# Attention sums with the weighted rows standing still and narrow one-hots moving, turned back in pairs of destination tiles

## The chip, the cores and the metric

The kernel runs on one core of one Trainium2 chip. The metric is the device time of one execution in microseconds (us). Engines are called by their names in the profile: PE (TensorE), with its weight loads as PEld, DVE (VectorE), ACT (ScalarE), POOL (GpSimd) and SP (SyncE). A measurement of this kernel is the median of several runs.

## What is computed

Four graph layers over 6,250 nodes and 100,000 edges, sorted by destination, each added to the running state. The change touches the third, an attention layer with eight heads, then a feed-forward network and two layer norms:

```python
h = (x @ W_gat).reshape(n, H, C)
a_s = jnp.sum(h * att_src, axis=-1); a_d = jnp.sum(h * att_dst, axis=-1)
e = a_s[src] + a_d[dst]
e = jnp.where(e >= 0, e, NEG_SLOPE * e)
m = jax.ops.segment_max(e, dst, num_segments=n)
alpha = jnp.exp(e - m[dst])
den = jax.ops.segment_sum(alpha, dst, num_segments=n)
alpha = alpha / den[dst]
agg = jax.ops.segment_sum(h[src] * alpha[..., None], dst, num_segments=n)
h1 = _layernorm(x + agg.reshape(n, H * C) + b_gat, ln1_g, ln1_b)
out = _layernorm(h1 + jax.nn.relu(h1 @ W1 + b1) @ W2 + b2, ln2_g, ln2_b)
```

What matters here is the last `segment_sum`: for every destination node the sum of its edges' weighted rows (128 numbers), of their eight weights, and, for the self-loop, the segment's maximum (eight more).

## The kernel before

The edges are cut into 782 tiles of 128 (`TILES`), the nodes into 49 tiles of 128 (`NT`). Since edges are sorted, a tile of 128 edges covers about eight nodes; the kernel allows each tile a reach of 26 to 64 nodes around its expected place (`reach_of`), and `near(tile)` lists the one or two node tiles that this reach touches. The attention goes in 56 batches (`ABATCHES`) of 14 edge tiles (`AB`), in two halves of seven (`AH`).

In one batch b the engines do this. POOL gathers the 14 tiles of source rows by indirect DMA into a ring of three batches (L1017); a slot is free again when the weighted rows of batch b-3 are made. SP loads per-edge flags (L694) and rows of destination numbers (L701). ACT copies the gathered scores into `stage` (L1286). PE turns them (L1876); DVE scans them forward and back for the segment maxima (L2550, L2551), PE fetches the neighbours across rows (L1887, L1888), DVE joins (L2555 to L2557), PE turns back (L1894, L1895). `expand` (L1809) brings node scores to the edges through one-hots made by `by_dst` (L2530, L2531), and DVE sums those pieces (L2561). Then DVE makes the exponents (L2567 to L2573), ACT the exponentials (L1325 to L1327), and DVE the weighted rows, 128 numbers a row (L2580), beside which lie the eight weights and eight maxima: 144 columns, `WL2`.

`by_edge` (L2538) makes, on DVE, for each edge tile a one-hot of 256 columns: the edge's destination modulo 256. It runs twice a batch, for seven tiles each. `aggregate` (L1828) on PE multiplies for each tile and each node tile near it: the 128 columns of the one-hot that belong to this node tile are loaded as the standing operand, the 144 columns of the weighted rows move, and the product (128 nodes by 144) adds up in bank `ps[i % 2]`. When the last edge tile near node tile i is through, ACT copies the sum to `Dw` (L1293, `agg_out`).

PE's order is written by hand: in the iteration of batch b it takes, for k from 0 to 13, the `expand` of tiles 2k and 2k+1 of batch b (for k under 7) and the `aggregate` of tile k of batch b-1. The fetch across rows stands behind k = 2, the turning back behind k = 5. So from k = 7 on an iteration holds `aggregate` alone, and DVE meanwhile makes exponents and weighted rows. DVE's order in a batch is: scans, joins, `by_edge` of half 0, the two sums of `expand`, exponents, `by_edge` of half 1, weighted rows, `by_dst` for the next batch, and then one or more steps of `residual`: for each group of seven node tiles (r = 0 to 6) a step called self, exp, mix, sum, stats, root, stand, norm, gain, one iteration after the other from iteration 8r+10 on. The feed-forward of finished groups runs within iterations 32 to 54 too (`FF_AT`). What is left of `residual` follows behind the last batch.

After the attention stand ten steps of the fourth layer, which the change does not touch.

## Time and profile before

| | us |
|---|---|
| median of 3 runs | 4953.56 |
| lowest and highest run | 4930.44, 4966.02 |
| span of the profiled execution | 6157.9 |
| the same, between first and last gather of the attention (L1017) | 1352.4 |

The profiled execution is 1204 us longer than the median run. Its rows give durations and who waits for whom; what a stretch takes in an execution that isn't profiled has to be argued. In the page's 40 slices the attention is 14 to 22; PE, DVE and POOL are each busy for about half of it. In the ten steps behind it PE stands at 8 tenths or more.

### The profile page before, as it was taken

To read this page: it belongs to the slowest core of one execution; us is meant where nothing else is said; L and a number is where in the kernel's file an instruction comes from. 1 tells how busy PE (TensorE), PEld (TensorE's weight loads), DVE (VectorE), ACT (ScalarE), POOL (GpSimd) and SP (SyncE) were. 2 spreads that over 40 slices of the span, in tenths; PEclk is the share of its full clock that TensorE was granted. 3 is DMA by queue.
4 is the path that set the end of the run, shared out by engine and by line. 5 is a ranking of instruction groups with operands and counts; after the bars stand their busy time and mean duration, and the time that the engine had idled before them with its cause. 6 is when DMAs were issued, how large, how long until landed. Compare 5 with 4: busy or idle time off the path is not lost.

```text
span 6157.9 us, 72323 instructions
## 1 busy us (share of the span) xinstructions
PE 4502.8 (73%) x25760; PEld 2814.8 (46%) x25760; DVE 2553.7 (41%) x8838; ACT 1022.9 (17%) x2922; POOL 3237.6 (53%) x3390
## 2 busy tenths in 40 slices
PE   3778477888775445446555788988888898888888
PEld 2556355566554334344444343434443444444344
DVE  6778444445443445555567422222222222222222
ACT  4656311111111000001222200000000000000001
POOL 3232365566555555555553365565656556565655
PEclk8888688899887666667767999989999999999999
DMA  5222222122222222222221555555555555555554
GB/s 136 77 83 79 77 56 52 51 58 59 55 55 57 67 70 75 68 68 69 65 71 42 160 173 159 171 158 164 172 167 164 166 178 166 161 174 161 165 170 135
DMA packets 455501, 686.46 MB, mean 111 GB/s; under 512 B 91793, under 2 KB 237879, under 8 KB 455120
## 3 DMA queue, kind: packets, MB, share of 16 engines
q1 hardware_dynamic: 341188, 454.71, 23.5%
q0 software_dynamic: 107584, 223.83, 14.0%
q8 instruction: 210, 3.44, 0.2%
q10 hardware_dynamic: 6364, 3.20, 0.2%
q14 instruction: 155, 1.27, 0.1%
HBM read 599.50 MB, written 82.31 MB: 111 GB/s over the span
## 4 chain that ended last, share of the span: by engine, by line
PE 42%; another core or an unknown queue 24%; DVE 18%; issue 11%; ACT 3%; DMA 1%; ACTq 0%; SPq 0%; DVEq 0%; POOL 0%; POOLq 0%
PE ps L2007 27%; PE ps L1751 5%; DVE E L2458 4%; DVE B L2538 2%; PE pt L2102 2%; DVE arena L2580 1%; PE ps L1828 1%; PE ps L2093 1%; PE pt L2038 1%; PE ps L2022 1%; DVE O L3023 1%; PE pt L1719 1%; ACT E L1561 1%; DVE scores L3019 1%
## 5 line engine op out<-in xcount | busy, mean ns | idle before, releaser
L2007 PE MATMUL ps<-arena,E 128*128 128x512 fp8e4 (+1 forms) x4900 | 1147.0, 385 | 93.6 <-issue 84.8
L2007 PE MATMUL ps<-arena,A 128*128 128x512 fp8e4 (+1 forms) x4900 | 1142.1, 385 | 62.4 <-issue 60.1
L1052 POOL DMA_INDIRECT arena<-table,src_i x810 | 776.9, 959 | 685.7 <-DMA table<-E 255.0
L1017 POOL DMA_INDIRECT E<-gat_table,src_i x782 | 759.3, 971 | 634.6 <-DVE arena L2580 367.7
L1052 POOL DMA_INDIRECT arena<-x_spill,src_i x810 | 775.3, 957 | 579.0 <-issue 225.8
L1002 POOL DMA_INDIRECT arena<-table,src_i x782 | 742.8, 950 | 583.5 <-issue 217.1
L1751 PE MATMUL ps<-E,arena 128*128 128x352 f32 (+22 forms) x2932 | 783.6, 421 | 241.1 <-DVE E L2458 155.4
L2007 PEld LDWEIGHTS ps<-arena,E 128*128 128x128 f16 x4900 | 471.4, 100 | 648.6 <-issue 193.9
L2007 PEld LDWEIGHTS ps<-arena,A 128*128 128x128 f16 x4900 | 472.9, 100 | 608.9 <-issue 154.8
L1751 PEld LDWEIGHTS ps<-E,arena 128*128 128x128 f32 x2932 | 515.4, 211 | 441.4 <-issue 195.5
L2909 DVE SCALAR_TENSOR_TENSOR C<-ps,sc_b,scores 128x128 f32<-128x128 f32 x490 | 138.9, 345 | 1295.1 <-PE ps L2022 769.3
L1828 PE MATMUL ps<-arena,B 128*128 128x144 f32 x2244 | 512.4, 376 | 62.4 <-issue 61.8
L2458 DVE SCALAR_TENSOR_TENSOR E<-arena,pt 128x512 f32<-128x512 bf16 (+5 forms) x782 | 480.6, 674 | 175.3 <-remote 85.7
L1828 PEld LDWEIGHTS ps<-arena,B 128*128 128x128 f32 x2244 | 415.1, 250 | 85.3 <-issue 83.1
L2102 PE MATMUL pt<-arena,E 128*128 128x258 f16 x1911 | 312.5, 286 | 67.8 <-ACT E L1561 45.2
L1087 POOL DMA_INDIRECT A<-first_rows,src_i x162 | 163.1, 1007 | 360.6 <-PE pt L2077 263.7
L1494 ACT ACTIVATE O<-ps 128x512 f32<-128x512 f32 x100 | 58.6, 586 | 1731.7 <-remote 920.3
L1561 ACT ACTIVATE E<-ps 128x490 fp8e4<-128x490 f32 (+1 forms) x507 | 299.0, 597 | 195.4 <-remote 122.2
L2895 DVE TENSOR_SCALAR rows<-w_gat,dst_f 128x54 f16<-128x54 bf16 (+17 forms) x966 | 155.5, 249 | 388.7 <-remote 251.4
L1876 PE MATMUL pt<-ident,E 128*128 128x128 f32 x56 | 23.9, 427 | 382.2 <-ACT E L1286 275.0
L3023 DVE TENSOR_SCALAR O<-arena 128x245 bf16<-128x245 bf16 x1014 | 233.4, 284 | 114.5 <-remote 75.0
L2093 PE MATMUL ps<-O,scores 128*128 128x245 bf16 x1014 | 201.2, 282 | 69.2 <-ACT E L1561 49.6
(350 smaller groups left out, 4557.6 us busy)
## 6 DMA issues: line engine op xcount, KB each, us to landing
arena<-adj SPq DMA_DIRECT2D x180, 1024.0 KB
arena<-adj SPq DMA_DIRECT2D x90, 1088.0 KB
adj<-E SPq DMA_DIRECT2D x39, 784.0 KB
arena<-table,src_i POOLq DMA_INDIRECT x1592
O<-dst_rows SPq DMA_DIRECT2D x112, 224.0 KB
arena<-adj SPq DMA_DIRECT2D x20, 768.0 KB
x_spill<-A SPq DMA_DIRECT2D x55, 256.0 KB
arena<-x_spill,src_i POOLq DMA_INDIRECT x810
```

Of the source, the lines that this page charges most:

```text
L1002: pool.indirect_dma_start(out=rows_ring[:, k % RING, :], out_offset=None, in_=table, in_offset=bass.IndirectOffsetOnAxis(ap=src_i[:, k:k + ...
L1017: pool.indirect_dma_start(out=att_rows[:, b % 3 * AB + at, :], out_offset=None, in_=gat_table, in_offset=bass.IndirectOffsetOnAxis(ap=src_ ...
L1052: pool.indirect_dma_start(out=y_rows[:, g % ERING, k, :], out_offset=None, in_=(table, x_spill)[half], in_offset=bass.IndirectOffsetOnAxis ...
L1087: pool.indirect_dma_start(out=rows0[:, x % (2 * EG0), :], out_offset=None, in_=first_rows, in_offset=bass.IndirectOffsetOnAxis(ap=src_i[:, ...
L1561: act.activation(made[:, i % MADE, :, 2 * BD * q:2 * BD * q + w], ps[pair % 4][:, 0:w * NT].rearrange("p (d j) -> p j d", j=NT), ACT.Copy, ...
L1751: mm = pe.matmul(ps[m % 4][:, (lo - WD * m) * BASES:(hi - WD * m) * BASES], rows_ring[:, k % RING, :], m_ring[:, k % MS, lo - first_dst(k) ...
L1828: mm = pe.matmul(ps[i % 2][:, 0:WL2], edge_hot[:, (2 * b + half) % 3, k % AH, i % 2 * P:(i % 2 + 1) * P], weighted_rows[:, b % 2, k, :], s ...
L2007: mm = pe.matmul(chunk_banks[n % 2][:, 0:len(some) * P], y[:, i, h * D:(h + 1) * D], adj_ring[:, piece % ADJ_RING, 0:len(some), at:at + P] ...
L2093: pe.matmul(ps[pair % 4][:, h * BW:(h + 1) * BW], hot_src[:, g % SRC, :], hot_code[:, g % HOT, 0:BW], start=True, stop=True).then_inc(sem( ...
L2102: mm = pe.matmul(bank0_of(m)[:, 0:2 * LO], made[:, m % MADE, j, :], y16[:, j, :], start=(j == 0), stop=(j == NT - 1))
L2458: dve.scalar_tensor_tensor(m_ring[:, k % MS, w, :], bc(iota_h[:, w], BASES), dst_rel[:, k:k + 1], row_bc(made_c[:, c % 2, at, :], w.stop - ...
L3023: dve.tensor_scalar(hot_code[:, g % HOT, 0:BW], iota_w[:, 0:BW], slot_c[:, g // P, g % P:g % P + 1], None, ALU.is_equal).then_inc(sem("hot ...
```

## The change

The product in `aggregate` is turned round. The weighted rows of an edge tile are now the standing operand, and a one-hot of at most 64 columns (`WD`), the window of destinations that the tile can reach, moves. It comes out as 128 features by at most 64 nodes, and 16 rows (weights and maxima) by as many nodes, which are two matmuls: one with the 128 feature columns standing (L1860 of the changed kernel) and one with the 16 columns beside them (L1864). Both are cut where the window crosses a boundary of 256 nodes (`window_parts`), since a bank of 512 columns now holds a pair of node tiles: columns 0 to 255 the features, columns 256 to 511 the 16 rows.

`by_edge` makes seven one-hots of 64 columns in one instruction (L2594) from `dst_in_window`, the destination relative to the window, which is copied once; before these were seven instructions of 256 columns.

When a pair is through, ACT copies the bank to SBUF in two pieces (`agg_keep`), PE turns it back in two or four transposes (`turn_back`, at k = 6 and k = 11) into `pt[0]`, and ACT copies 288 columns to `Dw` (`agg_out`). In all 25 pairs. The steps of `residual` all come one iteration later.

```diff
@@ buffers @@
-        edge_hot = B[:, 0:3 * AH * 2 * P].rearrange("p (s t d) -> p s t d", s=3, t=AH)
+        edge_hot = B[:, 0:3 * AH * WD].rearrange("p (s t d) -> p s t d", s=3, t=AH)
+        dst_in_window = B[:, 2048:2048 + ET]
+        agg_in, agg_beside_in = B[:, 3072:3072 + 2 * P], B[0:2 * HEADS, 3072 + 2 * P:3072 + 4 * P]
@@ helpers @@
+        def window_parts(tile):
+            lo, hi = max(reach_of(tile)[0], 0), min(reach_of(tile)[1], NP)
+            ends = [lo, *range(lo // (2 * P) * 2 * P + 2 * P, hi, 2 * P), hi]
+            return [(a // (2 * P), a % (2 * P), b - a, a - first_dst(tile)) for a, b in zip(ends, ends[1:])]
+
+        PAIRS = (NT + 1) // 2
+        pair_first, pair_last = ([end(k for k in range(TILES) if c in [part[0] for part in window_parts(k)])
+                                  for c in range(PAIRS)] for end in (min, max))
+
+        def pairs_ended(b, half):
+            return [c for c in range(PAIRS) if pair_last[c] // AB == b and pair_last[c] % AB // AH == half]
+
+        def pair_width(c):
+            return min(2, NT - 2 * c)
+
...
+        agg_back = pt[0][:, WL2:3 * WL2]
...
-        RESIDUAL = {"self": 10, "exp": 11, "mix": 12, "sum": 13, "stats": 14, "root": 15, "stand": 16, "norm": 17, "gain": 18}
+        RESIDUAL = {"self": 11, "exp": 12, "mix": 13, "sum": 14, "stats": 15, "root": 16, "stand": 17, "norm": 18, "gain": 19}
@@ ScalarE @@
+                def agg_keep(b, half):
+                    for c in pairs_ended(b, half):
+                        n = pair_width(c) * P
+                        act.wait_ge(sem("aggregated"), pair_last[c] + 1)
+                        if c:
+                            act.wait_ge(sem("agg_turned"), c)
+                        act.activation(agg_in[:, 0:n], ps[c % 2][:, 0:n], ACT.Copy)
+                        act.activation(agg_beside_in[:, 0:n], ps[c % 2][0:2 * HEADS, 2 * P:2 * P + n], ACT.Copy
+                                       ).then_inc(sem("agg_kept"), 1)
+
                 def agg_out(b, half):
-                    for i in range(NT):
-                        if near_last[i] // AB == b and near_last[i] % AB // AH == half:
-                            act.wait_ge(sem("aggregated"), near_last[i] + 1)
-                            act.activation(Dw[:, i * WL2:(i + 1) * WL2], ps[i % 2][:, 0:WL2], ACT.Copy
-                                           ).then_inc(sem("agg_out"), 1)
+                    for c in pairs_ended(b, half):
+                        n = pair_width(c) * WL2
+                        act.wait_ge(sem("agg_turned"), c + 1)
+                        act.activation(Dw[:, 2 * c * WL2:2 * c * WL2 + n], agg_back[:, 0:n], ACT.Copy
+                                       ).then_inc(sem("agg_out"), 1)
 
...
-                    agg_out(b - 1, 0)
+                    agg_keep(b - 1, 0)
                     if b < ABATCHES:
                         act.wait_ge(sem("exponents_made"), b + 1)
...
-                    agg_out(b - 1, 1)
+                    agg_out(b - 2, 1)
+                    agg_keep(b - 1, 1)
+                    agg_out(b - 1, 0)
...
+                agg_out(ABATCHES - 1, 1)
@@ TensorE @@
-                    for i in near(tile):
-                        if tile == near_first[i] and i >= 2:
-                            pe.wait_ge(sem("agg_out"), i - 1)
-                        mm = pe.matmul(ps[i % 2][:, 0:WL2],
-                                       edge_hot[:, (2 * b + half) % 3, k % AH, i % 2 * P:(i % 2 + 1) * P],
-                                       weighted_rows[:, b % 2, k, :],
-                                       start=(tile == near_first[i]), stop=(tile == near_last[i]))
+                    parts = window_parts(tile)
+                    for c, at, n, col in parts:
+                        if tile == pair_first[c] and c >= 2:
+                            pe.wait_ge(sem("agg_kept"), c - 1)
+                        pe.matmul(ps[c % 2][:, at:at + n], weighted_rows[:, b % 2, k, 0:D],
+                                  edge_hot[:, (2 * b + half) % 3, k % AH, col:col + n],
+                                  start=(tile == pair_first[c]), stop=False, skip_group_check=True)
+                    for c, at, n, col in parts:
+                        mm = pe.matmul(ps[c % 2][0:2 * HEADS, 2 * P + at:2 * P + at + n], weighted_rows[:, b % 2, k, D:WL2],
+                                       edge_hot[:, (2 * b + half) % 3, k % AH, col:col + n],
+                                       start=False, stop=(tile == pair_last[c]), skip_group_check=True)
                     mm.then_inc(sem("aggregated"), 1)
+
+                def turn_back(b, half):
+                    for c in pairs_ended(b, half):
+                        pe.wait_ge(sem("agg_kept"), c + 1)
+                        if c:
+                            pe.wait_ge(sem("agg_out"), c)
+                        for k in range(pair_width(c)):
+                            pe.transpose(agg_back[:, k * WL2:k * WL2 + D], agg_in[:, k * P:(k + 1) * P], ident[:, :])
+                            mm = pe.transpose(agg_back[:, k * WL2 + D:(k + 1) * WL2], agg_beside_in[:, k * P:(k + 1) * P],
+                                              ident[0:2 * HEADS, 0:2 * HEADS])
+                        mm.then_inc(sem("agg_turned"), 1)
+
+                def turned_by(b):
+                    return [c for v in range(b) for c in pairs_ended(v - 2, 1) + pairs_ended(v - 1, 0)]
 
...
+                        if turned_by(b):
+                            pe.wait_ge(sem("agg_out"), max(turned_by(b)) + 1)
...
                             aggregate(b - 1, k)
+                        if k == 6:
+                            turn_back(b - 2, 1)
+                        if k == 11:
+                            turn_back(b - 1, 0)
...
+                turn_back(ABATCHES - 1, 1)
@@ VectorE @@
+                link(dve.tensor_copy(dst_in_window, dst_rel))
...
-                    for k in range(AH):
-                        a = dve.tensor_scalar(edge_hot[:, g % 3, k, :], iota_y, dst_f[:, g * AH + k:g * AH + k + 1], None,
-                                              ALU.is_equal)
-                    a.then_inc(sem("by_edge"), 1)
+                    dve.tensor_tensor(edge_hot[:, g % 3, :, :], row_bc(iota_y[:, 0:WD], AH),
+                                      bc(dst_in_window[:, g * AH:(g + 1) * AH], WD), ALU.is_equal
+                                      ).then_inc(sem("by_edge"), 1)
 
...
-                dve.wait_ge(sem("agg_out"), NT)
+                dve.wait_ge(sem("agg_out"), PAIRS)
...
-                        dve.wait_ge(sem("agg_out"), (r + 1) * T7)
+                        dve.wait_ge(sem("agg_out"), (r * T7 + T7 - 1) // 2 + 1)
```

How the order moves. On PE, the end of one iteration in the middle of the attention; L1828 is `aggregate`, L1876 opens the next iteration, the last row is its `expand`. Before:

```order
L1828 MATMUL ps<-arena,B 128x144
L1894 MATMUL pt<-ident,E 128x128
L1895 MATMUL pt<-ident,E 128x128
L1809 MATMUL ps<-arena 128x48 x2
L1828 MATMUL ps<-arena,B 128x144 x9
L1876 MATMUL pt<-ident,E 128x128
L1809 MATMUL ps<-arena,B 128x48 x3
```

In the changed kernel (L1860 and L1864 are `aggregate`, L1927 is the old L1876, L1840 the old L1809):

```order
L1860 MATMUL ps<-B,arena 128x54
L1864 MATMUL ps<-B,arena 16x54
L1860 MATMUL ps<-B,arena 128x54
L1864 MATMUL ps<-B,arena 16x54
L1860 MATMUL ps<-B,arena 128x47
L1860 MATMUL ps<-B,arena 128x7
L1864 MATMUL ps<-B,arena 16x47
L1864 MATMUL ps<-B,arena 16x7
L1927 MATMUL pt<-ident,E 128x128
L1840 MATMUL ps<-arena,B 128x48 x3
```

Where one matmul stood per edge tile and node tile, two stand per edge tile and window part; the last tile shown crosses a boundary of 256 nodes and has four.

On DVE, behind the exponents (L2573) of one batch, up to its weighted rows (L2580) and the one-hots of the next (L2530). Before:

```order
L2573 TENSOR_TENSOR O<-O 128x112
L2538 TENSOR_SCALAR B<-w_gat,dst_f 128x256 x7
L2580 TENSOR_TENSOR arena<-E,pt 128x7x128 x2
L2530 TENSOR_SCALAR B<-O,part_n 128x896
L2531 TENSOR_SCALAR B<-O,part_n 128x896
```

In the changed kernel (L2594 is `by_edge`, L2636 the weighted rows, L2587 `by_dst`):

```order
L2629 TENSOR_TENSOR O<-O 128x112
L2594 TENSOR_TENSOR B<-w_gat,B 128x448
L2636 TENSOR_TENSOR arena<-E,pt 128x7x128 x2
L2587 TENSOR_SCALAR B<-O,part_n 128x896
L2588 TENSOR_SCALAR B<-O,part_n 128x896
```

Seven instructions have become one of 448 columns; nothing else on DVE has changed its place here.

On ACT, the copies of finished sums between the exponentials (L1325 to L1327) and the staging (L1286). Before, one node tile is copied as it ends (L1293):

```order
L1325 ACTIVATE arena<-pt 128x14x8
L1326 ACTIVATE pt<-O 128x112
L1327 ACTIVATE arena<-O 128x14x8
L1293 ACTIVATE arena<-ps 128x144
L1286 ACTIVATE E<-E 128x14x8
L1286 ACTIVATE E<-E 128x8 x2
L1325 ACTIVATE arena<-pt 128x14x8
L1326 ACTIVATE pt<-O 128x112
```

In the changed kernel a pair is copied out (L1313, L1314) ahead of the exponentials (L1353 to L1355), and its turned form (L1321) stands behind them, ahead of the next staging (L1304):

```order
L1313 ACTIVATE B<-ps 128x256
L1314 ACTIVATE B<-ps 16x256
L1304 ACTIVATE E<-E 128x14x8
L1304 ACTIVATE E<-E 128x8 x2
L1353 ACTIVATE arena<-pt 128x14x8
L1354 ACTIVATE pt<-O 128x112
L1355 ACTIVATE arena<-O 128x14x8
L1321 ACTIVATE arena<-pt 128x288
L1304 ACTIVATE E<-E 128x14x8
L1304 ACTIVATE E<-E 128x8 x2
```

So an iteration in which a pair ends has three copies where before it had one or none.

## Rows read from the trace of the kernel before

**Rows 1.** The page: busy us, share of the span, instructions.
```profile
span 6157.9 us, 72323 instructions
PE 4502.8 (73%) x25760; PEld 2814.8 (46%) x25760; DVE 2553.7 (41%) x8838; ACT 1022.9 (17%) x2922; POOL 3237.6 (53%) x3390
```

**Rows 2.** Windows: PE, PEld, DVE, ACT, POOL busy (instructions); clock; DMA share; GB/s.
```profile
2014.00:3362.00 1348.00, 695.15 (x4131) 599.31 (x4131) 756.21 (x2183) 163.34 (x551) 718.20 (x739) 0.67 0.27 68
...
2818.00:3319.00 501.00, 287.44 (x1678) 240.00 (x1678) 303.12 (x890) 95.60 (x272) 271.11 (x277) 0.70 0.27 68
3319.00:3400.00 81.00, 48.97 (x293) 38.83 (x293) 63.95 (x192) 32.65 (x75) 0.00 (x0) 0.79 0.11 37
3400.00:6158.00 2758.00, 2390.43 (x13802) 1142.32 (x13802) 693.42 (x3465) 230.10 (x665) 1552.17 (x1620) 0.94 0.53 165
```

**Rows 3.** Gathers by line: duration ns min/median/max, first and last start.
```profile
L1002 POOL DMA_INDIRECT arena<-table,src_i x782: 942/947/2756, 699.2 to 1914.7; - x196
...
L1017 POOL DMA_INDIRECT E<-gat_table,src_i x782: 942/947/1825, 1956.8 to 3309.2; - x196
```

**Rows 4.** Timeline, 2525 to 2592 us: POOL's gathers in an undisturbed row, and its wait.
```profile
2552.87 0.94 POOL L1017 DMA_INDIRECT E<-gat_table,src_i  x1 [0.30 <-issue]
2554.12 0.95 POOL L1017 DMA_INDIRECT E<-gat_table,src_i  x1 [0.30 <-issue]
...
2573.12 0.95 POOL L1017 DMA_INDIRECT E<-gat_table,src_i  x1 [16.80 <-DVE arena L2580]
```

**Rows 5.** Timeline, one batch that nothing held up (2561.15 to 2574.69 us).
```profile
2561.15 0.48 PE L1876 MATMUL pt<-ident,E 128*128 128x128 f32 x1 [25.34 <-ACT E L1286]
2564.66 0.36 DVE L2555 SCALAR_TENSOR_TENSOR E<-weight_e,pt,E 128x128 f32<-128x128 f32 x1 [2.07 <-PE pt L1888]
2565.66 1.92 DVE L2538 TENSOR_SCALAR B<-w_gat,dst_f 128x256 f32<-128x256 bf16 x7
2567.50 0.91 DVE L2561 TENSOR_REDUCE arena<-ps 128x112 f32<-128x336 f32 x2
2569.93 1.92 DVE L2538 TENSOR_SCALAR B<-w_gat,dst_f 128x256 f32<-128x256 bf16 x7
2571.77 2.08 DVE L2580 TENSOR_TENSOR arena<-E,pt 128x896 f32<-128x896 f32 x2
2574.69 0.27 PE L1809 MATMUL ps<-arena,B 128*128 128x48 bf16 x4 [1.72 <-DVE B L2531]
```

**Rows 6.** Timeline, a batch in which PE starts one matmul in 1.4 to 2.8 us.
```profile
2595.04 0.40 PE L1828 MATMUL ps<-arena,B 128*128 128x144 f32 x1 [1.83 <-issue]
2596.45 0.40 PE L1828 MATMUL ps<-arena,B 128*128 128x144 f32 x1 [1.00 <-issue]
2598.55 0.40 PE L1828 MATMUL ps<-arena,B 128*128 128x144 f32 x1 [1.70 <-issue]
...
2612.76 0.42 DVE L2550 TENSOR_TENSOR_SCAN E<-weight_e,pt 128x128 f32<-128x128 f32 x1 [20.21 <-remote]
```

**Rows 7.** Groups of instructions in the attention, 2020 to 3360 us: busy us, mean ns.
```profile
L1828 PE MATMUL ps<-arena,B 128*128 128x144 f32 x2226 | 508.6, 376 | 62.4 <-issue 61.8
L2538 DVE TENSOR_SCALAR B<-w_gat,dst_f 128x256 f32<-128x256 bf16 x770 | 224.8, 362 | 14.4 <-remote 14.1 <-PE ps L1828 0.2
L1293 ACT ACTIVATE arena<-ps 128x144 f32<-128x144 f32 x48 | 13.8, 288 | 384.3 <-PE ps L1828 206.5 <-remote 171.0 <-issue 6.8
L2662 DVE TENSOR_TENSOR C<-C,rows 128x512 f32<-128x512 f32 x5 | 3.5, 692 | 0.2
L2662 DVE TENSOR_TENSOR C<-C,rows 128x384 f32<-128x384 f32 x4 | 2.2, 558 | 0.1
L1315 ACT ACTIVATE arena<-pt 128x384 f32<-128x384 f32 x5 | 2.5, 491 | 42.3 <-remote 22.6 <-PE pt L1854 19.8
```

**Rows 8.** Timeline of PE: blocks of f32 matmuls; two lengths of one form give a pace.
```profile
1506.98 0.53 PE L1706 MATMUL pt<-arena 128*128 128x32 f32 x4
1512.53 1.95 PE L1719 MATMUL pt<-arena 128*128 128x128 f32 x16
...
1512.53 1.72 PE L1719 MATMUL pt<-arena 128*128 128x128 f32 x14
...
2562.34 0.83 PE L1828 MATMUL ps<-arena,B 128*128 128x144 f32 x2
2591.74 1.31 PE L1828 MATMUL ps<-arena,B 128*128 128x144 f32 x4
...
2574.81 0.74 PE L1828 MATMUL ps<-arena,B 128*128 128x144 f32 x4
2577.23 0.49 PE L1828 MATMUL ps<-arena,B 128*128 128x144 f32 x2
```

2 lines of the change are left out of this document (1 added, 1 removed).

## The prediction, made before the changed kernel was run

> **What bounds the kernel now.** I read the page first, then the windows by stage, the gathers, and one batch in the timeline. The profiled span is 6157.9 us [rows 1], the median run 4953.56: 1204 us fewer. So before anything is costed, it must be asked where the runs save this, and whether the attention, 1352 us from first to last gather in the profile [rows 3], is bound by the same thing there.
>
> In the attention nobody is busy: in 1348 us PE has 695, DVE 756, POOL 718 [rows 2]. Gathers that nothing holds up start every 1.25 us [rows 4], so 782 of them need 978 us, 17.5 us a batch of 14. That is a floor which the change does not touch. One batch that neither gather nor PE held up took from 2561.15 to 2574.69, 13.5 us [rows 5]: the loop of PE and DVE is quicker than POOL. Yet the profiled batch takes 24 us (1348/55.5), and POOL waits up to 16.8 us for weighted rows [rows 4]. The timeline shows why: in many batches PE starts one instruction in 1.4 to 2.8 us although nothing releases it ("issue"), and DVE stands 20 us behind it [rows 6]. The unhindered batch shows no such gap.
>
> How much of that is left in a run that isn't profiled? Compare floors. Behind 3400 us PE is busy 2390 of 2758 us at clock 0.94 [rows 2]; at most some 370 us can be saved there. The gathers of L1002 and L1017 span 1215 and 1352 us for 978 of floor each [rows 3], at most 240 and 375. Together 985. The remaining 220 of the 1204 must come from the first 699 us. So the runs save nearly all that the floors allow, or the floors are themselves lower there. Either way the attention takes about 1000 to 1050 us in a run, close to POOL's 978. I take POOL's gathers as its bound, with the loop of PE and DVE close below it.
>
> How close? In the unhindered batch DVE's one long wait is 2.07 us, for the fetch across rows [rows 5], so its own work there is some 11.4 us. In the whole stretch it averages 756/55.5 = 13.6, the rest being `residual`; in the 20 batches from 2818 to 3319 it is 303/20 = 15.2 [rows 2]. With about 2 of waits: 15.6 on average and 17.2 in the late batches, against 17.5. The ring of three batches evens out single heavy ones.
>
> **The change, part by part.**
>
> `by_edge` on DVE: seven instructions took 1.92 us [rows 5]. The one that replaces them has 448 columns in f32. From L2662, 558 ns for 384 columns and 692 for 512 [rows 7], it takes 0.63 us, so 1.29 less, 112 times: 144 us of DVE's busy time, 2.6 us a batch. If mixed types cost more, the upper end is the 1.92 that it replaces. Only the second of the two (2569.93, between exponents and weighted rows) is on the path; during the first, DVE would else wait for `expand`.
>
> `aggregate` on PE: each f32 matmul is two instructions in the profile, so 1122 matmuls are 2244. Their pace: (1.31-0.83)/2 = 0.24 us at the slow clock, (0.74-0.49)/2 = 0.125 at the fast one [rows 8], 539 or 280 us in all. The stretch had a granted clock of 0.67 [rows 2]. The change has 952 + 952 matmuls of on average 46 moving columns. Those with 128 standing columns don't gain from a third of the columns: f32 matmuls of 128 moving columns come every (1.95-1.72)/2 = 0.115 us, and four of only 32 took 0.53, 0.13 each [rows 8]. Something other than the moving columns sets this, and the load of 128 standing f32 columns is what both share. So 1904 instructions at 0.115 (0.23 slow, twice that) are 219 (438) us. For those with 16 standing columns there is no row. Lower bound, if only the 46 columns count: 0.125 x 46/144 = 0.04 (0.077 slow), 76 (146) us. Upper bound, if the load costs as with 128 columns: 219 (438). I take 0.05 (0.09), near the lower end, as a narrow load has an eighth of the columns: 95 (171). Sum 314 (609) against 280 (539): PE gets 34 to 70 us slower, 0.6 to 1.25 us a batch, and with the upper bound 158 to 337 us, 2.8 to 6 a batch. The change does not speed PE up.
>
> The Trainium skill (TensorE: Matmul & The Clock Gate, section on LDWEIGHTS) says that a load takes its columns over 1.2 ns, whatever the rows; for 128 columns that gives 107 ns, and the 0.115 of the rows agrees. For 16 columns it would give an estimate of 13 ns, which puts the matmuls beside at the lower bound and the sum at 295 us at the fast clock; no run here shows it yet.
>
> `turn_back`: 98 transposes, 196 instructions at 0.115 to 0.23: 23 to 45 us, 0.4 to 0.8 a batch. They stand at k = 6 behind `expand` and at k = 11, where PE has aggregation alone and in the unhindered batch ends 1.7 us before the next one-hots [rows 5]. What covers them is this slack; with DVE 1.3 quicker it is 0.4, and in a batch with a pair's end 0.5 to 1 us sticks out. `turn_back` waits for ACT's copy; behind it stand four or fewer `aggregate` tiles and the next batch's turn.
>
> ACT: 49 copies of 288 ns [rows 7] become 75, of 256 to 288 columns: 384 columns take 491 ns [rows 7], so some 0.4 each, 30 us against 14. `agg_keep` ahead of the exponentials hides in ACT's wait for exponents. Behind them `agg_keep` and `agg_out` stand ahead of the next staging, up to 1.2 us in a batch where before it was 0.3; they end before or with PE's last tile, so I cost them at 0, and 25 x 0.9 = 22 us if the loop were the bound and this cover gone.
>
> `residual` one iteration later: one step, of up to four or five DVE instructions of 896 columns, moves from inside the loop to the end: +3 us. The one-time copy of 784 columns: +1.
>
> **The sum.** With POOL as the bound the loop's gain is worth nothing in light batches. The loop goes from 13.5 by -1.29 + 0.6 (half of PE's loss) + 0.5 to about 13.3. In the some 22 late batches it goes from 17.2 to about 15.9 or less, where I count 0 to 15 us for what stood above 17.5 in single batches: -8. Behind the last gather two batches run out at the loop's pace: -1. Then +3 + 1. Sum -5 us. Against the profile's own span this is 6153, if its stalls stay; against the median of the runs 4953.6 it gives **4948 us**.
>
> **The rivals.** (1) The loop of DVE and PE is the bound, since gathers come faster when not profiled. For it: the floors above hardly leave room for 1204 us; against it: gathers start every 1.25 us with 0.30 between, wherever nothing holds them. Price: PE at the fast clock loses 0.3 in the phase that DVE waits for, so a light batch gains 1.0, a late one, DVE-bound, 1.5: 34 + 33 = 67 us, 4887 us. Chance 0.18. (2) Slower: the array has to empty when the standing operand changes between 128 and 16 columns, so that PE becomes the bound. There are two changes per edge tile, 1564, 28 a batch. Price of one: the next load lies bare, 0.115 to 0.23 us, so 3.2 to 6.4 us of PE a batch. PE's busy time is 287/20 = 14.4 in a late batch and (695-287)/35 = 11.7 in a light one [rows 2]; with the 1.2 above it comes to 18.8 to 22.0 and 16.1 to 19.3, against 17.5. That is 22 x 1.3 = 29 us at the one end and 22 x 4.5 + 34 x 1.8 = 160 at the other; I take 80: 5030 us. It decides from 0.07 us a change on (17.5 - 15.6 = 1.9, over 28). For it: nothing in the trace, where nearly every matmul has 128 standing columns. Against it: nothing either. Chance 0.12. (3) PE's issue, not its array, sets the pace: loads and matmuls of `aggregate` and `turn_back` go from 4488 to 8008. If the up to 70 us by which the attention may lie above its floor are issue time of its 8262 instructions [rows 2], 3520 more cost 30 us: 4983. Chance 0.08.
>
> The Trainium skill (TensorEngine Tiling, section Key Properties) has a rule for (2): changing the tiling mode drains the engine. Whether a matmul with 16 output rows changes the mode, no row here tells; by that rule the time would be that of (2).
>
> **How the numbers follow.** The forecast has 0.58, the rivals 0.18, 0.12, 0.08, and 0.04 is left for what I don't see. About 1% (50 us) is what a measurement of this kernel can tell from no change. Faster by over 1% is (1) and a little of the rest: 0.20. Slower by over 1% is (2) with an expensive change: 0.14. Within 1%: 0.66. The range goes from 4880, rival (1), to 5010; the dearer half of (2) lies outside.
>
> **What would show it.** L2594 at 0.6 us and 112 of them. L1860 at a pace of 0.115 fast; L1864 at 0.04 to 0.06; if its pace is that of L1860 or worse, the upper bound or (2) holds. The profiled attention may get longer than 1352 us, since PE's stalls there would grow with 3520 instructions more; that would say nothing on the runs by itself. POOL still waits for weighted rows in the profile. I am wrong if DVE's gain shows in the runs in full (over 50 us), for then POOL wasn't the bound, or if the runs get slower while PE's pace is as costed.

## The result and the profile after

| | us |
|---|---|
| changed kernel, median of 7 runs | 4997.53 (4983.31 to 5025.97) |
| kernel before, 7 runs of the same series | 4956.97 (4930.44 to 4977.65) |
| ratio, 95% interval | 1.0084 (1.0051 to 1.0117) |
| predicted | 4948, range 4880 to 5010, most likely no change that can be measured |

The change makes the kernel 0.84% slower, some 40 us. That is within 1%, and inside the range, but the interval leaves no doubt of the sign, and the forecast was a shift of -5 us.

The one profile of before that the prediction could read was an exceptional execution: 6157.9 us [rows 1], where the median run took 4953.56. So the kernel before was run once more, and its second profile has 4934.8 us. All profiles that follow have their run's normal length. One other execution of the kernel before, not profiled, was exceptional too: 7533.9 us at a mean granted clock of 0.673, beside 14 of 4930 to 4940 us at 0.915 to 0.920. Pages of before (second profile) and of after; busy us, share of the span, instructions, then the granted clock in 40 slices:

```profile
span 4934.8 us, 72323 instructions
PE 4186.1 (85%) x25760; PEld 2692.9 (55%) x25760; DVE 2561.4 (52%) x8838; ACT 1033.9 (21%) x2922; POOL 3249.5 (66%) x3390
...
PEclk9999689999997667777778999999999999999999
```

```profile
span 4995.6 us, 75050 instructions
PE 4532.7 (91%) x27422; PEld 2877.8 (58%) x27422; DVE 2389.4 (48%) x8167; ACT 1045.8 (21%) x2950; POOL 3295.0 (66%) x3390
...
PEclk9999789999997555557656999999999999999999
```

Of PE's 4502.8 us in [rows 1], 317 were part of the exceptional execution: in a normal one it is 4186.1. The change adds 347 us of PE and takes 172 off DVE. In the nine slices of the attention (13 to 21) the clock stands at 6 or 7 tenths before; after the change it is 5 in six of them.

Where the time is, two lines of each profile tell: the attention's gathers, and the first gathers of the next layer. Before (L1017, L1052), then after (L1035, L1070); duration ns, first and last start, and under the gathers of the attention what they waited for DVE's weighted rows (us, times):

```profile
L1017 POOL DMA_INDIRECT E<-gat_table,src_i x782: 943/947/1815, 1577.7 to 2584.0; - x196
...
  DVE arena L2580: 10.1, 12
...
L1052 POOL DMA_INDIRECT arena<-table,src_i x810: 942/947/1968, 2717.0 to 4693.6; - x162
```

```profile
L1035 POOL DMA_INDIRECT E<-gat_table,src_i x782: 938/944/1849, 1606.4 to 2629.7; - x196
...
  DVE arena L2636: 24.9, 20
...
L1070 POOL DMA_INDIRECT arena<-table,src_i x810: 940/944/1669, 2784.4 to 4754.8; - x162
```

From first to last gather 1006.3 us become 1023.3 (+17.0); from there to the next layer's first gather 133.0 become 154.7 (+21.7). I call the sum of both, first gather to first gather, the **attention**: 1139.3 before, 1178.0 after, +38.7, which is the whole of the 40 us. Behind it both need nearly the same: 4934.8 - 2717.0 = 2217.8 and 4995.6 - 2784.4 = 2211.2. The later first gather of after (1606.4) is no effect of the change: five altered kernels below start it at 1574.2 to 1577.1 and four of another series at 1610.3 to 1627.7, the grouped one with the earlier residual (ratio 0.9976) among them. All figures "attention" below are read from these two lines of the kernel named.

Two windows, one over the first 457 us from the first turn (some 25 batches), one over batches 32 to 53, by the starts of their turns (L1876, L1927). Columns as in [rows 2]:

```profile
1598.00:2055.00 457.00, 264.68 (x1696) 246.86 (x1696) 326.50 (x910) 47.27 (x188) 347.87 (x358) 0.69 0.38 95
2172.00:2586.00 414.00, 276.24 (x1824) 236.63 (x1824) 331.11 (x953) 106.37 (x296) 310.17 (x317) 0.77 0.36 91
```

```profile
1627.00:2085.00 458.00, 409.23 (x2382) 317.75 (x2380) 246.69 (x597) 48.39 (x195) 349.17 (x358) 0.50 0.38 95
2203.00:2640.00 437.00, 412.88 (x2487) 311.77 (x2487) 267.75 (x697) 114.58 (x309) 312.47 (x317) 0.62 0.36 89
```

The early batches are at POOL's pace in both: from the first turn to that of batch 14 it is 250.7 us before and 250.9 after, to that of batch 32 573.5 and 576.7. A granted clock of 0.50 is the lower of its two levels (1.2 GHz) all through, so after the change the early batches never leave it, and POOL still hides that. The 22 late ones go from 414/22 = 18.8 to 437/22 = 19.9 us each, and PE's busy time there goes from 12.6 to 18.8 us a batch. The gathers need 17.9 (14 of 1.28 on average), so PE is now above POOL's floor. The 18.8 of before were above it already, with PE at 12.6: in the late batches something longer than the gathers was there already, most likely the loop of PE and DVE (DVE alone 331.11/22 = 15.1 us busy, and its waits). Who waits for whom agrees. What the turn waited for, before (L1876) and after (L1927), us and times:

```profile
L1876 PE MATMUL pt<-ident,E x56: 328/474/478, 1598.5 to 2603.0; 128*128 128x128 f32 x56
...
  ACT E L1286: 703.0, 111
```

```profile
L1927 PE MATMUL pt<-ident,E x56: 327/477/477, 1626.8 to 2658.9; 128*128 128x128 f32 x56
...
  ACT E L1304: 166.3, 63
```

Before, PE stood at nearly every turn for rows just gathered, 703.0 us in all (loads and matmuls counted each). After it is 166.3: PE comes late to the turn itself. POOL in its place waits 24.9 us for weighted rows, 10.1 before (the rows of the gathers above). The last turn comes 19.0 us behind the last gather before and 29.2 after, so PE carries a backlog past the end of the gathers, behind which more than half of the loss lies.

### The profile page after: what moved, and what is told of

It is laid out like the page before. It is cut to its first block, busy times and chain, and to the rows that moved or that the text cites. A ratio compares the mean times of both kernels' runs of the same rounds, so it can differ in the third digit from the quotient of the medians.

```text
span 4995.6 us, 75050 instructions
## 1 busy us (share of the span) xinstructions
PE 4532.7 (91%) x27422; PEld 2877.8 (58%) x27422; DVE 2389.4 (48%) x8167; ACT 1045.8 (21%) x2950; POOL 3295.0 (66%) x3390
## 3 DMA queue, kind: packets, MB, share of 16 engines
q1 hardware_dynamic: 341188, 454.71, 29.2%
## 4 chain that ended last, share of the span: by engine, by line
PE 53%; POOL 25%; issue 9%; DVE 8%; DMA 3%; ACT 2%; SPq 0%; DVEq 0%; POOLq 0%; ACTq 0%
PE ps L2063 35%; POOL arena L1020 13%; POOL E L1035 6%; POOL arena L1070 4%; PE ps L1860 4%; DVE O L3079 2%; PE ps L1864 2%; POOL A L1105 2%; PE pt L2094 2%; DVE scores L3075 1%; PE ps L1782 1%; PE pt L1885 1%; PE ps L2078 1%; PE pt L1894 1%; DMA arena<-table,src_i 1%
## 5 line engine op out<-in xcount | busy, mean ns | idle before, releaser
L1070 POOL DMA_INDIRECT arena<-table,src_i x810 | 773.8, 955 | 472.5 <-issue 232.3
L2063 PE MATMUL ps<-arena,E 128*128 128x512 fp8e4 (+1 forms) x4900 | 1077.7, 374 | 7.8 <-DMA arena<-adj 7.8
L2063 PE MATMUL ps<-arena,A 128*128 128x512 fp8e4 (+1 forms) x4900 | 1077.5, 374 | 0.0
L1070 POOL DMA_INDIRECT arena<-x_spill,src_i x810 | 770.7, 952 | 328.0 <-issue 232.9
L1035 POOL DMA_INDIRECT E<-gat_table,src_i x782 | 767.3, 981 | 282.7 <-issue 232.0
L1782 PE MATMUL ps<-E,arena 128*128 128x352 f32 (+22 forms) x2932 | 734.4, 401 | 120.1 <-DMA arena<-table,src_i 119.4
L1782 PEld LDWEIGHTS ps<-E,arena 128*128 128x128 f32 x2932 | 488.3, 200 | 294.9 <-DMA arena<-table,src_i 145.1
L1860 PE MATMUL ps<-B,arena 128*128 128x64 f32 (+17 forms) x1904 | 545.4, 397 | 0.0
L1860 PEld LDWEIGHTS ps<-B,arena 128*128 128x128 f32 x1904 | 441.1, 298 | 64.1 <-issue 48.3
L1105 POOL DMA_INDIRECT A<-first_rows,src_i x162 | 221.5, 1367 | 203.3 <-PE pt L2133 105.2
L2158 PE MATMUL pt<-arena,E 128*128 128x258 f16 x1911 | 296.4, 275 | 1.4 <-ACT E L1592 1.4
L1864 PE MATMUL ps<-B,arena 128*16 128x64 f32 (+17 forms) x1904 | 277.4, 256 | 0.0
L1247 ACT ACTIVATE arena<-ps 128x512 f32<-128x512 f32 x98 | 58.5, 597 | 746.3 <-PE ps L1782 746.3
```

What stands on the lines that cost most here:

```text
L1035: pool.indirect_dma_start(out=att_rows[:, b % 3 * AB + at, :], out_offset=None, in_=gat_table, in_offset=bass.IndirectOffsetOnAxis(ap=src_ ...
L1070: pool.indirect_dma_start(out=y_rows[:, g % ERING, k, :], out_offset=None, in_=(table, x_spill)[half], in_offset=bass.IndirectOffsetOnAxis ...
L1105: pool.indirect_dma_start(out=rows0[:, x % (2 * EG0), :], out_offset=None, in_=first_rows, in_offset=bass.IndirectOffsetOnAxis(ap=src_i[:, ...
L1782: mm = pe.matmul(ps[m % 4][:, (lo - WD * m) * BASES:(hi - WD * m) * BASES], rows_ring[:, k % RING, :], m_ring[:, k % MS, lo - first_dst(k) ...
L1860: pe.matmul(ps[c % 2][:, at:at + n], weighted_rows[:, b % 2, k, 0:D], edge_hot[:, (2 * b + half) % 3, k % AH, col:col + n], start=(tile == ...
L1864: mm = pe.matmul(ps[c % 2][0:2 * HEADS, 2 * P + at:2 * P + at + n], weighted_rows[:, b % 2, k, D:WL2], edge_hot[:, (2 * b + half) % 3, k % ...
```

## The experiments

Ratios are to the kernel before in the same series. PE is the busy us of the late window over its 22 batches, clock the granted clock of that window (bounds by each kernel's own turns). Attention: first gather to first gather of the next layer.

| kernel | ratio (95%) | attention | PE a late batch | clock late |
|---|---|---|---|---|
| before | 1 | 1139.3 | 12.6 | 0.77 |
| changed | 1.0084 (1.0051 to 1.0117) | 1178.0 | 18.8 | 0.62 |
| changed, again | 1.0119 (1.0078 to 1.0160) | 1178.4 | 18.8 | 0.62 |
| narrow ones in groups of 7 tiles | 0.9982 (0.9972 to 0.9991) | 1131.0 | 14.2 | 0.71 |
| narrow ones in pairs of tiles | 1.0006 (0.9992 to 1.0019) | 1144.6 | 16.1 | 0.68 |
| no narrow ones | 0.9984 (0.9960 to 1.0008) | 1125.0 | 12.4 | 0.67 |
| all standing operands wide | 1.0103 (1.0087 to 1.0118) | 1196.0 | 18.5 | 0.64 |
| before with a narrow pair | 1.0055 (1.0039 to 1.0070) | 1153.4 | 16.5 | 0.86 |
| changed, 128 columns moving | 1.0008 (0.9999 to 1.0018) | 1145.2 | 16.4 | 0.82 |
| changed, DVE's one-hots three times | 1.0121 (1.0105 to 1.0136) | 1199.2 | 19.2 | 0.61 |
| groups of 7, DVE three times | 1.0010 (0.9987 to 1.0032) | 1144.1 | 14.9 | 0.68 |
| groups of 7, residual not later | 0.9976 (0.9951 to 1.0002) | 1131.3 | 14.5 | 0.70 |
| before, residual later | 0.9982 (0.9973 to 0.9991) | 1135.2 | 12.6 | 0.79 |

Two theories stood against each other. **PE**: `aggregate` costs more than it did, by the changes between 128 and 16 standing columns or by loads that cost alike whatever their width, and passes POOL's floor. **Hand-over**: PE's work is hidden, and what costs is the chain `agg_keep`, `turn_back`, `agg_out` and the later residual behind the last batch.

### The kernel before once more

Nothing is edited; a second profile of before.

> The kernel before, profiled a second time. If the stalls of its first profile (PE starting one instruction in 1.4 to 2.8 us) belong to that one execution, the span is now near 4955 us, the attention takes 1000 to 1030 us from first to last gather, and POOL never waits long for weighted rows in the light batches. PE theory (the changed kernel is slower because PE became the bound of the attention): PE is busy at most 15 us a batch here, against 17.6 (batches 14 to 31) and 18.7 (32 to 54) in the changed kernel, and the late batches take 17.5 to 18.5 us against its 19.8. Handoff theory (it is slower through ACT's copies, the turning back and the later residual): PE's busy time a batch is about the same in both.

One run, 4936.94 us, profile above. The stalls of [rows 6] are gone, the attention's gathers take 1006.3 us where they took 1352 [rows 3].

### Narrow matmuls in groups (e1_grouped)

```diff
-                    for c, at, n, col in parts:
-                        mm = pe.matmul(ps[c % 2][0:2 * HEADS, ...
-                    mm.then_inc(sem("aggregated"), 1)
+                    if k % AH == AH - 1 or tile == TILES - 1:
+                        for j in range(half * AH, k + 1):
+                            for c, at, n, col in window_parts(b * AB + j):
+                                mm = pe.matmul(ps[c % 2][0:2 * HEADS, ...
+                            mm.then_inc(sem("aggregated"), 1)
```

The same matmuls, in another order: seven tiles' wide ones, then seven tiles' narrow ones, four changes a batch in place of 28.

> The changed kernel with the matmuls of 16 standing columns taken together behind the seven edge tiles of a half, so that PE changes between 128 and 16 standing columns 4 times a batch and not 28. In the changed kernel a main matmul ahead of one of 16 columns takes 350 ns to the next start and not 231, and the one of 16 columns ahead of a main one 222 and not 67: 0.27 us for two changes at the slow clock. PE theory with bare loads: 12 pairs of changes fewer in a batch, 3.3 us less of PE, late batches back at 17.5 to 18, time 4997 - 25 to 45 = 4952 to 4972 us. Handoff theory: no change, 4990 to 5005 us, or slower, since the finished sums come at the end of a half.

Measured 0.9982: the loss is gone, 12 us less than before in medians, and more is gained than the 25 to 45 us expected. The matmuls, the copies, the turning back and the late residual are all still there, so the hand-over theory falls with this one run. In PE's timeline one tile without a cut, at the slow clock, is two products with 128 standing columns and two with 16. Changed kernel, then grouped (start, us):

```profile
1780.44 0.67 PE L1860 MATMUL ps<-B,arena 128*128 128x54 f32 x2
1781.04 0.36 PE L1864 MATMUL ps<-B,arena 128*16 128x54 f32 x2
1781.33 0.67 PE L1860 MATMUL ps<-B,arena 128*128 128x54 f32 x2
```

```profile
1795.65 1.44 PE L1866 MATMUL ps<-B,arena 128*16 128x54 f32 x14
1797.02 3.24 PE L1860 MATMUL ps<-B,arena 128*128 128x54 f32 x14
1800.19 1.52 PE L1866 MATMUL ps<-B,arena 128*16 128x54 f32 x14
```

Changed: from start to start 1781.33 - 1780.44 = 0.89 us a tile. Grouped: 1800.19 - 1795.65 = 4.54 for seven, 0.65 a tile. Grouping seven tiles takes away 12 of their 14 changes: (7 x 0.89 - 4.54)/12 = 0.14 us a change, not the 0.12 of the expectations, which divided the 0.24 between the tiles by two.

```profile
1595.00:2050.00 455.00, 336.45 (x2399) 314.10 (x2397) 249.56 (x605) 51.76 (x197) 346.19 (x358) 0.50 0.38 96
2167.00:2570.00 403.00, 312.20 (x2484) 269.01 (x2484) 266.43 (x695) 117.66 (x310) 308.20 (x312) 0.71 0.38 94
```

The instructions of the late window are the same in number (2484 and 2487), PE's time is 312.20 for 412.88: 4.6 us a batch fewer. Of these the 24 changes taken away are 24 x 0.14 = 3.4 at the slow clock; the rest goes with the higher clock, 0.71 for 0.62.

### In pairs of tiles (e11_pairs)

The same edit with two tiles a group: 16 changes a batch.

> The changed kernel with the second matmuls taken together for two edge tiles: 16 changes of width a batch, where the changed kernel has 28 and e1_grouped 4. Bare-change theory: 12 changes fewer at 0.12 us each are 1.5 us of PE a batch, about half of the way to e1_grouped (PE 17.6 -> 16 in batches 14 to 31, 19.8 -> 18.8 us a late batch), ratio 1.001 to 1.006. If grouping helped e1_grouped for another reason (the later count of finished tiles), pairs would give nothing: 1.008 to 1.012.

1.0006, PE 16.1: between the two on each count (14.2 with four changes, 18.8 with 28). PE is below the floor of 17.9, and nearly the whole loss is gone already, more than expected (1.001 to 1.006, PE 18.8). From here to the groups of seven another 0.24% is gained, with PE below the floor in both: the larger part of the loss goes when PE's total passes the floor, but not all of it.

### No narrow matmuls (e4_no_beside)

```diff
-                    for c, at, n, col in parts:
-                        mm = pe.matmul(ps[c % 2][0:2 * HEADS, ...
+                    if tile in pair_first:
+                        c = pair_first.index(tile)
+                        mm = pe.matmul(ps[c % 2][0:2 * HEADS, 2 * P:4 * P], ...
```

One narrow product of 256 columns is left where a pair begins; the sums of the weights and maxima are left out.

> The changed kernel without the second matmuls (16 standing columns) except one of 256 columns where a pair begins; the sums of weights and maxima are therefore left out. PE theory: an edge tile without a cut takes 2 x 0.235 = 0.47 us at the slow clock and not 0.90 to 0.95, PE falls from 17.6 and 18.7 us a batch (batches 14 to 31, 32 to 54) by 17 x 0.4 = 6 to 8 us, far under POOL's 17.9, and the attention runs at the pace of the gathers: as e1_grouped or a little under, 4915 to 4930 us beside 4937 of before. If it stays above 4960, PE is not the cause.

0.9984, attention 1125.0, the shortest of all. PE's 12.4 us a late batch are the level of before (12.6). The clock is not: 0.67 for 0.77 in the late batches, and 0.50 for 0.69 in the first 457 us, with PE busy 278.58 us there, where before had 264.68. So the clock is lower with hardly a change of width too. What remains different on PE is how few columns the wide products move, and the turning back. In time the run gains less than expected: 4964.25 us by the median, in a series where before has 4967.89.

### All standing operands with 128 columns (e2_wide)

```diff
-                        mm = pe.matmul(ps[c % 2][0:2 * HEADS, 2 * P + at:2 * P + at + n], weighted_rows[:, b % 2, k, D:WL2],
+                        mm = pe.matmul(ps[c % 2][:, 2 * P + at:2 * P + at + n], weighted_rows[:, b % 2, k, 2 * HEADS:WL2],
```

The 16 columns are loaded with the 112 ahead of them, so there is no change of width, but twice the wide loads; copy and turning back take the last 32 rows.

> The changed kernel with 128 standing columns in the second matmul too (the last 128 of the 144), of which rows 96 to 127 are copied and turned back. There are no changes of width any more, but each second matmul loads 128 columns. Bare-change theory: all matmuls then come at an even 0.235 us (slow clock), an edge tile without a cut takes 4 x 0.235 = 0.94 us against 0.90 to 0.95, so PE and the time stay as they are: 4990 to 5010 us. If the number of standing columns itself were what is cheap about the second matmul (0.067 x 2) and no change cost anything, this would add 2 x 0.17 x 17 = 5.7 us a batch of PE and 100 us or more in all. Handoff theory: no change.

1.0103, as slow as the changed kernel. A tile:

```profile
1785.47 0.65 PE L1860 MATMUL ps<-B,arena 128*128 128x54 f32 x2
1785.92 0.63 PE L1864 MATMUL ps<-B,arena 128*128 128x54 f32 x2
1786.34 0.43 PE L1949 MATMUL pt<-ident,E 128*128 128x128 f32 x1
```

0.45 + 0.42 = 0.87 us, against 0.89 with changes. Dropping the changes gains as much as the two loads that are now wide lose (each matmul is two instructions, so a tile has four, two of them wider than before). So the run doesn't refute the cost of a change. It shows that the kernel sits at the prediction's upper bound whichever way it is paid.

### A narrow pair added to the kernel before (e9_before_narrow)

```diff
+                    pe.matmul(ps[near(tile)[-1] % 2][0:2 * HEADS, 2 * P:2 * P + 48], weighted_rows[:, b % 2, k, D:WL2],
+                              edge_hot[:, (2 * b + half) % 3, k % AH, 0:48], start=False, stop=(tile in near_last),
+                              skip_group_check=True
+                              ).then_inc(sem("aggregated"), 1)
```

The old order and tiling, and behind each tile one more matmul with 16 standing and 48 moving columns, whose product nobody reads.

> The kernel before with one more matmul behind each edge tile's aggregation, 16 standing and 48 moving columns, whose product nobody reads: two changes between 128 and 16 standing columns per edge tile, as in the changed kernel, beside the old wide products. Bare-change theory: such a tile costs PE 2 x 0.06 for the columns and some 0.27 for the two changes at the slow clock, 0.4 x 14 = 5.5 us a batch; PE goes from 10.8 and 12.6 (batches 14 to 31, 32 to 54) to 15.5 to 18, and the time grows by 5 to 30 us, most of it in the late batches. If changes cost nothing, PE grows by 1.5 to 2 us a batch and the time by 0 to 5.

1.0055: a narrow pair alone brings a loss into the old kernel, of 0.55% where the change has 0.84%. PE is at 16.5 us a late batch, below the gathers' 17.9, so here the loss is not PE over POOL's floor. In its profile the attention is 14.1 us longer than before: the late batches go from 18.8 to 19.1 us, though the first and last gather lie only 3.1 us further apart, and 11.0 stand behind the last gather. DVE still has its old work (329.42/22 = 15.0 us a late batch), and most likely PE's added time comes on top of it in the loop of the two. At the slow clock:

```profile
1996.34 0.83 PE L1828 MATMUL ps<-arena,B 128*128 128x144 f32 x2
1997.09 0.34 PE L1832 MATMUL ps<-B,arena 128*16 128x48 f32 x2
1997.37 0.34 PE L1809 MATMUL ps<-arena 128*128 128x48 bf16 x4
```

Two products of 144 columns took 0.48 when others of the kind followed [rows 8]; ahead of a narrow one they take 1997.09 - 1996.34 = 0.75, so the change costs 0.27 here, nearly twice what it costs behind 54 moving columns (two products take 0.60 ahead of a narrow one in the changed kernel, 0.45 in the grouped, 3.17 / 7: 0.15, or 0.17 when the one change in the 3.17 is taken out).

### 128 columns moving (e10_wide_moving)

```diff
-                        pe.matmul(ps[c % 2][:, at:at + n], weighted_rows[:, b % 2, k, 0:D],
-                                  edge_hot[:, (2 * b + half) % 3, k % AH, col:col + n],
+                        lo = min(k % AH * WD, AH * WD - P)
+                        pe.matmul(ps[c % 2][:, min(at, P):min(at, P) + P], weighted_rows[:, b % 2, k, 0:D],
+                                  edge_hot[:, (2 * b + half) % 3, :, :].rearrange("p t d -> p (t d)")[:, lo:lo + P],
```

This run is on the clock. Grouping had raised it along with saving the changes; here all 28 changes stay, and only the wide products move 128 columns in place of up to 64. The columns beyond the window are a neighbouring tile's, so the kernel leaves out the right sums of the features.

> The changed kernel with 128 columns of the one-hots moving in each main matmul in place of at most 64; the sums of the features are therefore wrong, the work of every other engine is the same. At the slow clock a matmul with 128 standing f32 columns starts every 0.213 us with 128 moving columns (e2_wide shows 0.213 for either), so wider ones cost PE nothing there. Clock theory: the changed kernel sits at a granted clock of 0.50 in batches 0 to 24, where the kernel before has 0.69 and e9_before_narrow 0.72 with PE as busy, because its products are narrow; wider ones bring the clock to 0.7 or more, PE's busy time falls from 17.6 us a batch to 15 or less, and the time goes down by 20 to 40 us, to a ratio of 0.999 to 1.006. If the width of what moves has no part in it: clock 0.50 to 0.56, PE 17.6 to 18.5, ratio 1.008 to 1.014.

1.0008: the loss against before is gone a second way, though not the 0.26% that the grouped kernel has besides. Windows of this kernel, and of before with the narrow pair:

```profile
1598.00:2055.00 457.00, 433.66 (x2330) 304.62 (x2330) 243.71 (x590) 45.49 (x191) 347.81 (x359) 0.52 0.38 94
2178.00:2579.00 401.00, 361.07 (x2488) 255.74 (x2488) 263.91 (x693) 115.53 (x309) 306.84 (x309) 0.82 0.37 94
```

```profile
1598.00:2055.00 457.00, 382.14 (x2367) 273.46 (x2367) 325.69 (x908) 45.75 (x187) 347.77 (x359) 0.72 0.38 96
2169.00:2590.00 421.00, 362.00 (x2440) 258.49 (x2440) 329.42 (x956) 106.06 (x295) 310.21 (x317) 0.86 0.36 90
```

In the late window the granted clock is 0.82 with 128 columns moving and 0.62 with up to 64, though PE does more. PE's time falls to 361.07 us (16.4 a batch), below the floor. A tile at the full clock, PE's timeline of this kernel and of the changed one:

```profile
2301.47 0.47 PE L1861 MATMUL ps<-B,arena 128*128 128x128 f32 x2
2301.87 0.28 PE L1865 MATMUL ps<-B,arena 128*16 128x64 f32 x2
2302.09 0.22 PE L1840 MATMUL ps<-arena,B 128*128 128x48 bf16 x2
```

```profile
2301.33 0.43 PE L1860 MATMUL ps<-B,arena 128*128 128x64 f32 x2
2301.70 0.28 PE L1864 MATMUL ps<-B,arena 128*16 128x64 f32 x2
2301.91 0.43 PE L1860 MATMUL ps<-B,arena 128*128 128x64 f32 x2
```

It is 0.62 us with 128 columns and 0.58 with 64, so at the full clock the wider product costs next to nothing. At the slow clock it costs more, against the expectation: from 1788.30 to 1789.32 us this kernel takes 1.02 us a tile, where the changed one has 0.89. The early window stays at 0.52 where 0.7 or more was expected, and PE there is busy 433.66 of 457 us, 24 more than in the changed kernel. Why the clock rose late and not early I can't say from these runs, so that the number of moving columns alone sets it isn't shown.

### DVE's one-hots three times (e3_dve_three, e6_grouped_dve_three)

```diff
-                    dve.tensor_tensor(edge_hot[:, g % 3, :, :], ...
+                    for again in range(3):
+                        a = dve.tensor_tensor(edge_hot[:, g % 3, :, :], ...
```

It gives back to DVE most of what the change took off it: 138 of the 172 us by the pages (2527.1 us busy for 2389.4).

> The changed kernel with the instruction that makes seven one-hots given three times (same result), which puts back 1.24 us of DVE each time, 2.5 us a batch, the work that the change took from DVE. PE theory: DVE is busy 12.1 us of 19.8 in late batches and not the bound, but the one-hots of half 1 lie on the way from expand to weighted rows; the time grows by 0 to 15 us, to 4997 to 5012. If the loop through DVE is the bound: 1.24 us of each of 56 batches, 5050 to 5070 us.

> e1_grouped with the instruction for the one-hots given three times, 2.5 us of DVE a batch put back. What does DVE's saving bring once PE is not the bound? POOL as the bound: light batches keep 17.8 to 17.9 us, late ones go from 18.1 back to at most the 18.7 of the kernel before, so + 0 to 15 us on e1_grouped: 4925 to 4940. If the loop through DVE sets the pace of every batch: + 1.24 x 56 = + 70 us, 4995.

In the changed kernel 1.0121, against 1.0084 and 1.0119 without: no difference that the intervals separate, though the one profile has 21 us more in the attention. In the grouped kernel 1.0010 against 0.9982, some 14 us, with intervals that still overlap a little (from 0.9987 and up to 0.9991); the attention is 13.1 us longer. So DVE's saving is worth some 14 us at most in the grouped kernel, and in the changed one nothing that the medians tell.

### The residual's place (e7_grouped_ten, e8_before_eleven)

```diff
-        RESIDUAL = {"self": 11, "exp": 12, "mix": 13, "sum": 14, "stats": 15, "root": 16, "stand": 17, "norm": 18, "gain": 19}
+        RESIDUAL = {"self": 10, "exp": 11, "mix": 12, "sum": 13, "stats": 14, "root": 15, "stand": 16, "norm": 17, "gain": 18}
```

That is the edit to the grouped kernel; the other run makes the opposite one in the kernel before.

> e1_grouped with the steps of residual one iteration earlier, as in the kernel before (from iteration 8r+10). The way from the last batch's turn to the first gather of the next layer took 114 us before and 121 in e1_grouped; a step less behind the last batch should give that back: -3 to -7 us, 4918 to 4922 us beside 4925. Against it: the step self then waits for ACT's copy of a pair that ends in the same iteration, four times, 1 to 3 us each in iterations where the loop has slack. If nothing changes, the later residual cost nothing.

> The kernel before with the steps of residual one iteration later (from 8r+11), the one part of the change that touches neither PE's products nor the one-hots. The sum of the prediction gave it + 3 us; e1_grouped against e0_before_again has 7 us more between the last turn and the next layer's first gather. Expected: + 3 to 7 us, a ratio of 1.0006 to 1.0014. If it is 0 within the interval, the later residual is no part of the loss.

In the grouped kernel the earlier place makes no difference that can be measured (0.9976, attention 1131.3 against 1131.0). In the kernel before, the later place gains 0.18%, 8 us by the medians, where I had put +3. Its gathers span 1001.2 us for 1006.3, its end 134.0 for 133.0, so the gain lies among the batches. POOL there waits 1.5 us for weighted rows where it waited 10.1, which fits, but one profile of each is too little for 5 us.

### The changed kernel once more (e5_changed_again)

> The changed kernel itself, on the chip of the other runs of this call. Expected from its first ratio, 1.008, and from e2_wide and e3_dve_three: 4975 to 5000 us. It is the base for what e3_dve_three and e2_wide added.

1.0119, attention 1178.4: the loss and its place repeat, in another series. The median is 5015.97 us, above the 4975 to 5000 expected; in this series the kernel before too is slower, 4967.89 for 4936.58, so only ratios are compared across series.

## Why the prediction was wrong, step by step

**Stalls and POOL's floor: right in the main.** The normal execution needs 1006.3 us between first and last gather, the prediction had 1000 to 1050. The early batches stand at POOL's pace before and after. The floor is 17.9 a batch, not 17.5: gathers come every 1.28 us on average, not 1.25 [rows 4], some being longer. Wrong for the late batches: they took 18.8 us before the change, where the text had the loop at 17.2 and the gathers as the bound.

**DVE's saving is worth little: right.** The new instruction takes 0.618 us (0.63 was costed) and there are 112; DVE's busy time falls by 172 us, and the kernel gets slower. The gain of 8 us that I saw in the late batches may be in the grouped kernel, where PE is out of the way: they take 403/22 = 18.3 for 18.8 us, 11 us in all, of which 6 go again with DVE's instruction given three times (408.5 us).

```profile
L2594 DVE TENSOR_TENSOR B<-w_gat,B x112: 612/618/677, 1630.4 to 2673.9; 128x448 f32<-128x448 bf16 x112
...
L1864 PEld LDWEIGHTS ps<-B,arena x1904: 92/103/152, 1645.4 to 2696.1; 128*16 128x16 f32 x191
```

**PE's price of `aggregate`: this step failed.** The matmuls with 16 standing columns were taken at 0.05 us (0.09 slow) each, "near the lower end, as a narrow load has an eighth of the columns". Among themselves they do run at some 0.09 to 0.10 slow (14 in 1.37 us, with one change in it). But no two tiles' narrow ones stand together in the changed kernel, and with the changes a narrow pair costs 0.89 less two wide ones of 0.226 (3.17 us for 14): 0.22 each, where the upper bound had 0.23. PE a late batch rose by 6.2 us, turning back included, where the sum had up to +1.25 for `aggregate` and 0.8 for turning back, and the upper bound's end for `aggregate` alone was 6. That number stood in the text, with the row that had PE at 14.4 in a late batch; at 12.6, as the normal execution has it, 12.6 + 6 is still over the floor. The lower value was chosen on the width of the load alone; nothing in the trace spoke for it, and I should have made the sum at both ends and seen that the floor lies between them.

**Rival (2), the change of width: the right mechanism with too small a chance.** Two changes cost 0.28 us a tile at the slow clock, 0.14 each, in the 0.115 to 0.23 that it gave; its lower end, +29 us, is close to the +40 found, and its deciding point (0.07 a change) was passed. It had a chance of 0.12. That its lower end puts PE at 18.8 us a late batch, just what was measured, is luck: it started from 14.4, out of the exceptional profile, and added 4.4, where the normal execution has 12.6 and the change added 6.2. The rule of the Trainium skill (TensorEngine Tiling, section Key Properties) was named for it, that changing the tiling mode drains the engine. The extra 0.27 us behind 144 moving columns and 0.15 to 0.17 behind 54 would fit an array that empties before it takes the other width. But the loads with 16 columns also begin only with their own product, so a load that isn't hidden would read alike, and no run separates the two. The Trainium skill's rule (TensorE: Matmul & The Clock Gate, section on LDWEIGHTS), by which the prediction estimated 13 ns for such a load, isn't borne out by the row above: 92 ns at the least, 103 in the median. But the same view has 186 to 338 ns for a load of 128 columns, where the rule gives 107, so at either width the profile's durations hold more than the rule counts, and how much of a narrow load lies bare no row tells.

**The clock was taken as unchanged: a second failure.** Prices at either clock were in the sum, but the share of each was taken from before. It fell from 0.69 to 0.50 in the early and from 0.77 to 0.62 in the late batches. The run with 128 moving columns shows what that was worth: with all changes in place and the clock at 0.82, nothing is lost against before. So in the changed kernel two things together carry PE over the floor by 0.9 us a batch, and taking away most of the changes or raising the clock brings it 1.5 or more below. Being over the floor is not the only way to lose: in the kernel before, with DVE's old work, the changes cost 0.55% at a clock of 0.86 and with PE at 16.5. And what lowers the clock is only in part shown: fewer moving columns go with it in the late batches, but 128 columns didn't raise it in the early ones.

**The end behind the last gather: not priced.** The text had two batches running out at the loop's pace, -1 us. It was +21.7: 10 from PE's backlog at the last turn, and 11.5 behind it. Of these some 7 are there in the grouped kernel too (from last turn to next layer 2705.2 - 2584.1 = 121.1, before 2717.0 - 2603.0 = 114.0), and with the earlier residual too (2742.2 - 2619.2 = 123.0). But in the kernel without narrow matmuls, which has the same copies and the same turning back, it is 2752.7 - 2636.1 = 116.6, only 2.6 above before. So most of the 7 go with the narrow matmuls of the last batch, and at most some 3 are left for the hand-over; one profile of each doesn't fix so small a number.

**ACT at 0 and the residual at +3.** The copies cost nothing that shows, since the grouped kernel has them all and is faster than before. The residual's sign was wrong. The 196 instructions costed for turning back are 98: a transpose is one instruction here (PE's count rises by 1662, 1564 for `aggregate` and 98). The one for the 128 features and the one for the 16 rows beside take 0.62 us together at the slow clock (0.41 and 0.21), 30 us for the 49 pairs, within the 23 to 45 of the sum.

**Rivals (1) and (3)** fell: DVE's gain never appeared, and the grouped kernel issues as many instructions more as the changed one, without loss.

Of the versions run, the grouped one (0.9982), the same with the earlier residual (0.9976) and the kernel before with the later one (0.9982) are the best, and not told apart. All three stand close to POOL's gathers, 782 of 1.28 us.

## What to carry to other kernels

Turning a product so that fewer columns move doesn't make it cheaper where something other than the moving columns sets the pace: at the slow clock two f32 instructions with 128 standing columns took 0.45 us with 54 moving columns and 0.48 with 144. Here the turn made 1.43 products a tile into 2.43. Where a design needs a second, narrower standing operand, put its matmuls together in groups: the same instructions took 0.89 us a tile in turn and 0.65 in groups of seven. And where a cost is unknown between two ends, put both into the busy sum of each engine and compare with the bound's floor: if the floor lies between them, the engine is a main case and not a rival at 0.12.
